# Latent scores: the keys' low parts against 64 rows of queries, one head in each half of the array

## The reference

```python
q = (x @ W_q).reshape(B, S, N_HEADS, D_HEAD).transpose(0, 2, 1, 3)
latent = x @ W_kv_down
kv = (latent @ W_kv_up).reshape(B, S, N_HEADS, D_HEAD).transpose(0, 2, 1, 3)
scores = jnp.einsum('bhqd,bhkd->bhqk', q, kv) * scale
probs = jax.nn.softmax(scores, axis=-1)
out = jnp.einsum('bhqk,bhkd->bhqd', probs, kv)
```

## Time and profile before

| | |
|---|---|
| time, median of three runs | 1693.83 us (1692.1 to 1697.16) |
| span of the profiled execution | 1695.7 us (no other time of it is given) |
| PE (matmuls) busy | 1441.4 us, 85% |
| PEld (weight loads) busy | 990.9 us, 58% |
| DVE busy | 1075.4 us, 63% |
| ACT busy | 750.3 us, 44% |
| POOL busy | 773.8 us, 46% |
| L2131, scores with the high parts | 256 matmuls, 490 ns each by the records |
| L2132, scores with the low parts | 256 matmuls, 395 ns each by the records |

### The profile page before, as it was taken

One profiled execution on the slowest core, in us unless ns is written; L12 is line 12 of the kernel. 1 busy time (PEld: TensorE's weight loads), 2 busy tenths in 40 slices (PEclk: granted clock), 3 DMA queues, 4 the chain that ended last, 5 costly groups with the idle time before them and its releaser, 6 DMA issues. The chain is left out here.

```text
span 1695.7 us, 39494 instructions
## 1 busy us (share of the span) xinstructions
PE 1441.4 (85%) x14334; PEld 990.9 (58%) x14334; DVE 1075.4 (63%) x2743; ACT 750.3 (44%) x1786; POOL 773.8 (46%) x741
## 2 busy tenths in 40 slices
PE   6879999448889996888999478877899999998799
PEld 3556656414545554455566356654677777777687
DVE  6852222457876564783222388876998888874888
ACT  5533333254555633553333311125776666752322
POOL 4453332763320000454333466606998888973000
PEclk9989999569999998899999788888999999999899
DMA  8309995631110002514999232200000000000000
GB/s 265 98 14 267 284 266 150 204 96 38 38 38 1 1 1 67 152 40 123 280 296 259 73 87 84 78 4 13 3 16 3 12 7 3 16 3 3 10 19 22
DMA packets 92664, 145.50 MB, mean 86 GB/s; under 512 B 25032, under 2 KB 52528, under 8 KB 92512
## 3 DMA queue, kind: packets, MB, share of 16 engines
q1 hardware_dynamic: 62816, 93.06, 19.1%
q0 software_dynamic: 15360, 37.77, 7.7%
q10 hardware_dynamic: 14336, 12.59, 2.7%
HBM read 122.39 MB, written 18.87 MB: 83 GB/s over the span
## 5 line engine op out<-in xcount | busy, mean ns | idle before, releaser
L2298 POOL TENSOR_TENSOR sb_m_prob<-sb_m_prob,sb_m_rinv 128x512 f32<-128x512 f32 x256 | 260.1, 1041 | 44.6 <-DVE sb_m_rinv L2348 40.8
L1272 POOL DMA_INDIRECT sb_c_rows<-slot_rows,sb_slot x192 | 192.1, 1000 | 102.7 <-issue 51.2
L2228 ACT ACTIVATE sb_m_prob<-m_ps_s,sb_m_nmax 128x512 f32<-128x512 f32 x256 | 173.8, 683 | 125.8 <-DVE sb_m_nmax L2354 125.2
L1106 POOL DMA_INDIRECT e_xn<-xn_rows,sb_table x128 | 117.7, 920 | 209.6 <-PE e_ps_x L1184 197.2
L1255 DVE TENSOR_TENSOR sb_e_h<-sb_e_sg,e_ps_gu 96x176 f32<-96x176 f32 x128 | 42.6, 333 | 256.5 <-ACT sb_e_sg L1231 256.5
L1193 PE MATMUL e_ps_gu<-e_wgu,sb_e_xT 128*96 128x352 f32 x512 | 178.1, 470 | 17.0 <-ACT sb_e_xT L1225 15.6
L2354 DVE TENSOR_REDUCE sb_m_nmax<-m_ps_s 128x1 f32<-128x512 f32 x256 | 163.8, 681 | 28.1 <-PE m_ps_s L2132 25.7
L2362 DVE STREAM_TRANSPOSE sb_m_pT<-sb_m_prob 128x1024 f32<-128x1024 f32 x128 | 157.5, 1232 | 0.0
L2145 PE MATMUL m_ps_v<-sb_m_pT,sb_m_lat_rows 32*64 32x128 f32 x8192 | 136.1, 275 | 4.6 <-issue 3.8
L2131 PE MATMUL m_ps_s<-sb_m_latT_high,sb_m_qa 128*128 128x512 f32 x256 | 125.5, 490 | 16.0 <-ACT sb_m_prob L2228 15.9
L2145 PEld LDWEIGHTS m_ps_v<-sb_m_pT,sb_m_lat_rows 32*64 32x64 f32 x8192 | 120.2, 131 | 27.8 <-issue 27.4
(11 more groups left out here) (280 smaller groups left out, 3076.4 us busy)
## 6 DMA issues: line engine op xcount, KB each, us to landing
e_wgu<-wgu SPq DMA_DIRECT2D x128, 352.0 KB, 4.9
e_wdn<-wdn SPq DMA_DIRECT2D x128, 192.0 KB, 4.7
slot_rows<-sb_e_y ACTq DMA_DIRECT2D x128, 96.0 KB
xn_rows<-e_xn SPq DMA_DIRECT2D x16, 256.0 KB, 2.2
sb_c_rows<-slot_rows,sb_slot POOLq DMA_INDIRECT x192, 2.8
sb_x<-x SPq DMA_DIRECT2D x4, 512.0 KB, 5.4
e_xn<-xn_rows,sb_table POOLq DMA_INDIRECT x128, 5.3
sb_g_zm<-wqT SPq DMA_DIRECT2D x1, 2048.0 KB, 9.1
```

What stands on the lines that cost most here:

```text
L1106: pool.indirect_dma_start(x, None, k.xn_rows[:, :], bass.IndirectOffsetOnAxis(ap=k.table[:, e:e + 1], axis=0))\
L1272: pool.indirect_dma_start(rows[u][j][:, :], None, k.slot_rows[:, :], bass.IndirectOffsetOnAxis(ap=k.slot[:, n, j:j + 1], axis=0))\
L2228: act.activation(prob[s % 4][:, hh, :], ps_s[j % 3][:, :], ACT.Exp, bias=nmax[s % 2][:, hh:hh + 1], accum_out=rsum[s % 2][:, hh:hh + 1]).t ...
L2298: pool.tensor_tensor(part, part, rinv[s % 2][:, hh:hh + 1].to_broadcast([P, T]), ALU.mult)\
```

## The change

In each step the two products with the high parts are now issued first, one for each head with its wait for the bank, and the two products with the low parts behind them. A low product takes only the 64 rows of its head's high query parts (`rows_of(hh)`) and the same 64 rows of the low latent; the product of the low query parts with the low latent parts falls away. Head 0 works in rows 0 to 63 of the array, head 1 in rows 64 to 127, and the two add into different PSUM banks. Each low product signals `s_ready` as before.

```diff
                     if j >= 3:
                         pe.wait_ge(p_ready, j - 2)
                     pe.matmul(ps_s[j % 3][:, :], q[:, hh, cols], latT[b % 2][0][:, :], start=True, stop=False)
-                    pe.matmul(ps_s[j % 3][:, :], q[:, hh, cols], latT[b % 2][1][:, :], start=False, stop=True).then_inc(s_ready, 1)
+                for hh in range(2):
+                    rows = rows_of(hh)
+                    pe.matmul(ps_s[(2 * s + hh) % 3][:, :], q[rows, hh, cols], latT[b % 2][1][rows, :],
+                              start=False, stop=True).then_inc(s_ready, 1)
```

## The result

The changed kernel takes 1720.67 us, the median of four runs (1715.9 to 1728.61); the kernel before took 1692.96 beside it. The ratio is 1.0163, with a 95% interval of 1.0129 to 1.0197: slower by 27.7 us, where the forecast was 16 and the range ended at 1729.

The account below looks back on a forecast made before the run. TensorE was taken to set the latent attention's pace except around 19 waits for an exponential. Step costs 11.7 plus waits 6.2, less 1.5 and 0.8, gave +15.6 us on the 1693.83 median: 1709, range 1688 to 1729.

Parts of the forecast that it names:

- the rival of the serial load: Each step's second low load waits for the first, 0.11 a step: +13, 1722; non-overlap in all has chance 0.09.
- The changes of tile: Two per step, 0.21 us each (0.10 draining, 0.11 bare load); with the saved stream, 11.7 us over 128 steps.
- x+0.56: x is the start of a step's first high product; both low loads were forecast 0.56 us after it.
- the four steps: Latent-attention steps from 1481.76 to 1495.06 in the last batch: 13.30 us before, forecast about 13.6.
- The waits: TensorE's 13 waits for an exponential behind 1181 us: 0.48 more each through the reordering, 6.2 us.
- The sum without the clock: Latent attention: 11.7 + 6.2, less 1.5 for steps 0 to 7 and 0.8 under DVE's cover: +15.6 us.
- The missing term: the clock: Granted clock in the latent stage: a fall from 0.99 was named as a sign of being wrong, without size.
- No price for the change of tile: Rival: low pair's weights are pulled ahead and nothing drains in the steps: -17.6 us, 1676; chance 0.17.
- The pair does not overlap: Rival: in each step the second low load (+13, 1722) or second stream (+28, 1737) waits; chance 0.09.
- Half the price: Rival: the steps' 0.11 loads hide beneath the draining, the 0.10 drains stay: -2 us, 1692; chance 0.10.

Follow-up runs that it names:

- the old order with four changes in a step: Kernel before with 64-row low products, each still directly behind its head's high product: 1768.54 us, ratio 1.0445.
- The order alone: Changed kernel's issue order, but low products keep all 128 rows, against the kernel before: 1700.54 us, ratio 1.0047.
- the second profile of before: The kernel before run once more, unchanged, for a second profile: 1697.56 us in one run, stage 381.5 us.
- the filled one: At first use: kernel before, first head's high product issued three times more in 19 idle steps, 1695.63 us; afterwards the filled kernel.
- the filled kernel: Changed kernel with the first head's high product issued four times more in the 19 steps where TensorE idled longest: 1706.42 us, ratio 1.0069 to before.

## Why the prediction was right in direction and short in size

The forecast's own band, 1702 to 1718, missed the 1720.67. The time lies inside the range only because the range was drawn to 1729 for the rival of the serial load, which the runs refute: that it holds the result is luck.

**The changes of tile: right.** The two changes of tile in a step cost what the rows at the values' edges said. The low loads were forecast at x+0.56 and came at +0.55; the next load 0.44 behind and came 0.43 behind; the four steps went from 13.30 to 13.59, for "about 13.6". For 64 rows this had rested on one weak row; now 128 of 128 steps show the gap, and the old order with four changes in a step met its forecast of 16.0 with 16.04. The rule of the Trainium skill, TensorEngine Tiling (Array Packing), section Key Properties, that a change of the tiling mode drains the engine, holds here for 128 to 64 rows and back; the trace adds 0.10 us for the draining and 0.11 for the load that can no longer hide.

**The waits: right.** From the second high product to the values 0.87 for 0.88, the four steps from 36 to 40 take 11.57 for 10.80, 0.77 more, where the forecast's terms for these steps add to 0.82. The order alone, without changes of tile, costs 6.6 to 7.8 us at the waits, for 6.0 expected of it. There are 16 such waits behind the opening of the stage and not 13.

**The sum without the clock: right in size.** +15.6 was forecast; with the low clock out of the way the stage is 15.5 us longer than in the first profile of before, 16.7 than in the second and 17.3 than in the filled one; these two have no low clock either. The times say it more loosely: the ratio of 1.0069 is 11.7 us, and its interval reaches from 5.6 to 18.0.

**The missing term: the clock.** The forecast kept the granted clock at 0.99 and named its fall only among the things that would prove it wrong; nothing in the sum stands for it. It fell to 0.96, and that cost 13.7 us, the difference between the changed kernel and the filled one. The same order without 64-row tiles idles as long at these waits (24.0 us against 23.2) and keeps the clock at 1.00 in its one profile; the filled kernel has the 64-row tiles, idles 5.1 us and keeps it too. So in the changed kernel it took both: take away either, and the clock stays. As a rule for other kernels that is not shown, for each can do it alone: the kernel before, with no scores on 64 rows, lost the clock once in two profiles, at 1169 us behind waits of 0.93, 1.13 and 0.98 us, and the 64 rows in the old order lost it behind a stretch in which PE's records cover 3.27 of 3.30 us. The waits in question, in the order alone and in the filled kernel (columns as in the earlier trace rows):

```profile
PE m_ps_s L2131 <- ACT sb_m_prob L2230: 24.0, 22, 1.8
```

```profile
PE m_ps_s L2134 <- ACT sb_m_prob L2234: 5.1, 19, 0.5
```

Which part of the 64-row products counts, the drains or the half-used array, no run here tells apart.

**The rivals.** "No price for the change of tile" (1676) fell: the load is not pulled ahead. "The pair does not overlap" (1722 to 1737) fell too, though the time lies near it: the two low loads of a pair stand in one row of 0.19 us, at one start, and with both products on one half the four steps take 0.92 us more. "Half the price" (1692) fell with 13.59. That the measured 1720.67 is near the price of a serial load is chance; the next loads' places show it.

## What to carry to other kernels

Using half the array for a product saves a stream, but each place where the tile changes has a price: in a stretch of 128-row matmuls, a pair of 64-row products saved 0.23 us and paid an estimated 0.42 for two drains and two bare weight loads. Where values, and so a change of tile, followed anyway, saving and price were about even (13.26 for 13.30 in four steps). A pair with work of its own tile on both sides was not run. Look in the trace for a place where the tile already changes, read the start-to-start distance and the bare load there, and count how many new places the edit makes. And where a TensorE-paced stage has waits, price them twice: once in idle time and once in the clock that may fall behind them. Here the clock cost 13.7 us, nearly as much as all the rest.

## What was not expected of the hardware

More TensorE work made the kernel faster: repeating products with no use, 76 of them at 0.23 us in idle time, took 13.7 us off the changed kernel's stage, because the granted clock stayed at 1.00. And a single halt of TensorE put down to "issue" lies in the midst of a block of values in each profile that was looked at for it: 0.53 us in step 96 of the kernel before, 0.83 at the same matmuls of the same step in the changed kernel, 0.80 in step 36 of the second profile of before. The order alone has halts at the same records of the same two steps (0.72 and 0.21 us), so among these kernels the place repeats and the length does not. What it is stays open; it is in both kernels and too small to bear on the difference.
